# A decoder block over 32 batches: the first LayerNorm's x is loaded already turned, its row statistics go through DRAM to all partitions, GpSimd applies them a batch ahead, and the steps of a batch stand in a new order

## The reference, cut to what matters

```python
# x: (32, 224, 512), ctx: (32, 750, 512); all weights 512 x 512 unless said
def _layernorm(x): return (x - mean(x)) / sqrt(var(x) + 1e-5)       # over the last axis, no weights
def attn(x):                                                        # 16 heads of 32
    q = x @ Wq.T / sqrt(512); k = x @ Wk.T; v = x @ Wv.T
    return concat_heads(softmax(q k^T) v) @ Wff.T + bff
def xattn(ctx, q):  ...  # one head over 750 rows of ctx
def ffn(h):         ...  # routing to 2048 keys, top 8, gathered values, a learned gate
x = x + attn(_layernorm(x))
x = x + xattn(ctx, _layernorm(x))
x = x + ffn(_layernorm(x))
```

## Time and profile before

| what | value |
|---|---|
| median of 3 runs | 2862.47 us (2859.62 to 2865.25) |
| the profiled execution, its time | 2859.07 us |
| the same, from its first to its last instruction (span) | 2857.2 us |
| busy: TensorE, VectorE, ScalarE, GpSimd | 2649.0, 2104.9, 1421.1, 785.7 us |
| mean granted clock of TensorE | 0.973 of full speed |

### The profile page before, as it was taken

The page is one execution under the profiler, slowest core; times in us unless marked ns, Lnnn a source line. Parts: engine busy times, 40 slices in busy tenths (PEclk is TensorE's granted clock), DMA queues, the critical chain, the costliest instruction groups (busy, mean ns, idle before and its releaser), DMA issues.

```text
span 2857.2 us, 53958 instructions
## 1 busy us (share of the span) xinstructions
PE 2649.0 (93%) x18042; PEld 1983.5 (69%) x18042; DVE 2104.9 (74%) x4071; ACT 1421.1 (50%) x4214; POOL 785.7 (27%) x651
## 2 busy tenths in 40 slices
PE   6899999999999999999999999999999999999830
PEld 4667777777777777777777777777777777777610
DVE  4446778878777788877777878777788877777652
ACT  2345554445455444555554445455544455555343
POOL 0001323222223232222323222223232222233245
PEclk9999999999999999999999999999999999999965
DMA  5112323333333332333323333333332333333799
GB/s 167 57 57 76 103 91 118 103 102 105 107 101 100 102 120 86 108 107 109 103 91 116 110 96 104 107 101 104 99 120 89 107 107 110 101 93 108 180 237 181
DMA packets 102683, 313.05 MB, mean 110 GB/s; under 512 B 14577, under 2 KB 15089, under 8 KB 94417
## 3 DMA queue, kind: packets, MB, share of 16 engines
q1 hardware_dynamic: 54002, 180.37, 19.2%
q0 software_dynamic: 48640, 132.16, 17.4%
HBM read 269.35 MB, written 43.12 MB: 109 GB/s over the span
## 4 chain that ended last, share of the span: by engine, by line
PE 90%; issue 2%; DVE 2%; DMA 2%; ACT 1%; POOL 1%; SPq 1%; POOLq 0%; DVEq 0%; ACTq 0%
PE psX L985 45%; PE psA L985 19%; PE psF L985 8%; PE psA L994 8%; PE psA L1072 4%; PE psA L1049 4%; PE psX L994 3%; DMA vg<-in_L_ffn_aux_values,idx 1%; DVE xT_lo L775 1%; PE psF L994 1%; ACT xT_hi L567 1%; POOL out L540 1%; POOL vg L523 0%; SPq L371 0%; ACT paT L550 0%
## 5 line engine op out<-in xcount | busy, mean ns | idle before, releaser
L523 POOL DMA_INDIRECT vg<-in_L_ffn_aux_values,idx x512 | 516.5, 1009 | 1635.1 <-DVE agg L890 830.9
L586 ACT ACTIVATE pa<-psA,nmax 112x224 f32<-112x224 f32 x1024 | 443.6, 449 | 150.3 <-DVE nmax L794 147.6
L890 DVE SCALAR_TENSOR_TENSOR agg<-vg,wt,agg 112x512 f32<-112x512 f32 x420 | 367.5, 875 | 16.2 <-DMA vg<-in_L_ffn_aux_values,idx 2.9
L794 DVE TENSOR_REDUCE nmax<-psA 112x4 f32<-112x896 f32 x256 | 266.7, 1083 | 149.8 <-PE psA L1049 149.8
L985 PE MATMUL psX<-big,gT 128*112 128x375 f32 x1024 | 333.4, 478 | 1.3 <-ACT nx L622 1.0
L985 PE MATMUL psX<-pT,cx 125*128 125x224 f32 x1536 | 307.5, 357 | 0.0
L550 ACT COPY paT<-psA 112x448 f32<-112x448 f32 x512 | 236.5, 544 | 111.1 <-PE psA L994 108.7
L985 PEld LDWEIGHTS psX<-pT,cx 125*128 125x128 f32 x1536 | 285.5, 190 | 7.7 <-issue 0.3
L807 DVE TENSOR_TENSOR pa<-pa,rsum 112x896 f32<-112x896 f32 x256 | 279.5, 1092 | 8.8
L985 PEld LDWEIGHTS psX<-big,gT 128*112 128x112 f32 x1024 | 177.4, 176 | 127.1 <-ACT nx L622 1.2
L985 PE MATMUL psX<-m,xnxT 128*112 128x512 f32 x512 | 235.6, 603 | 0.0
(11 more groups left out here) (195 smaller groups left out, 5301.5 us busy)
## 6 DMA issues: line engine op xcount, KB each, us to landing
big<-in_ctx_t SPq DMA_DIRECT2D x32, 1500.0 KB, 6.7
cx<-in_ctx SPq DMA_DIRECT2D x32, 1500.0 KB
xa<-in_x SPq DMA_DIRECT2D x32, 448.0 KB, 4.7
xr<-in_x SPq DMA_DIRECT2D x32, 448.0 KB, 3.9
out<-x SPq DMA_DIRECT2D x32, 448.0 KB, 3.1
agg_scratch<-agg SPq DMA_DIRECT2D x60, 224.0 KB, 6.4
vg<-in_L_ffn_aux_values,idx POOLq DMA_INDIRECT x512, 3.7
over_weights<-agg_scratch SPq DMA_DIRECT2D x15, 448.0 KB, 13.5
```

The costliest lines, as they stand in the source:

```text
L523: pool.indirect_dma_start(vg[:, c % SLOTS, k, :], None, aux_values, bass.IndirectOffsetOnAxis(ap=idx[:, t, n:n + 1], axis=0))\
L586: last = nc.scalar.activation(pa[:, t, h, :], psA[0:R, h, t * S:(t + 1) * S], ACT.Exp, bias=nmax[:, k % 2, h, t:t + 1], accum_out=rsum[:, ...
L794: nc.vector.tensor_reduce(nmax[:, k % 2, h:h + 2, :], psA[0:R, h:h + 2, 0:T * S].rearrange("p h (t s) -> p h t s", t=T), AX_X, ALU.max, ne ...
L890: last = nc.vector.scalar_tensor_tensor(dst, vg[:, c % SLOTS, k, :], w, dst, ALU.mult, ALU.add)
```

## The change

- x is passed a second time, turned: `in_x_t`, per batch 128 partitions x 896 (four chunks of 224 rows). SyncE loads it into a new buffer `centered`.
- A new stream N works on batch i + 1. ("N", "norm"): VectorE's statistics as before, without the last two operations (centring and scaling 112x512); then two small copies put mean and inverse root into `moments`, which SyncE stores to DRAM. ("N", "spread"): SyncE loads these 448 numbers into all 128 partitions (`spread`). ("N", "center"): GpSimd subtracts the mean and multiplies by the inverse root over 128x896 values, in place, ScalarE writes the high part and VectorE the low part, one operation each.
- TensorE's turn of `xa` is gone, and with it two fills. So that the fills stay a multiple of four, ("A", "value") now has four: each is 12 matmuls with 256 columns instead of 512.
- `ORDER` is new. A list `FIRST` puts ahead of iteration 0: norm and spread of batch 0, the split of Wq, its centring, then the split of Wk and Wv, then the keys. Iteration 30 is unrolled too.

```diff
-    ("A", "norm", 0), ("X", "enter", 0), ("A", "turn", 0), ("G", "sum", 0), ("X", "norm", 0), ("A", "qk", 0),
...
+    ("G", "sum", 0), ("X", "enter", 0), ("X", "norm", 0), ("A", "qk", 0), ("A", "value", 0), ("G", "sum", 1),
...
-FILLS = {("A", "turn"): 2, ("A", "qk"): 1, ("A", "value"): 2, ("A", "score"): HB, ("A", "prob"): 2 * T,
+FILLS = {("A", "qk"): 1, ("A", "value"): 2 * T, ("A", "score"): HB, ("A", "prob"): 2 * T,
...
+FIRST = (("N", "norm", 0), ("N", "spread", 0), ("W", "split", 0), ("N", "center", 0), ("W", "split", 1),
+         ("W", "split", 2), ("W", "keys", 0), ("W", "keys", 1), ("W", "keys", 2), ("W", "keys", 3))
...
+            def store_moments(b, _):
+                sp.wait_ge(moments_ready, b + 1)
+                sp.dma_start(row(moments_dram, b), moments[:, :, :].rearrange("p t k -> p (t k)")).then_inc(moments_stored, 16)
+                if not (isinstance(b, int) and b == B - 1):
+                    sp.dma_start(xa[:, :, :], tiles(row(x, b + 1))).then_inc(x_loaded, 16)
+
+            def spread_moments(b, _):
+                sp.wait_ge(moments_stored, 16 * (b + 1))
+                wait(sp, xt_scaled, b)
+                sp.dma_start(spread[:, :], row(moments_dram, b).rearrange("r k -> (r k)").partition_broadcast(P))\
+                    .then_inc(moments_spread, 16)
...
+            def center(b, _):
+                mean, rstd = (spread[:, :].rearrange("p (r t k) -> p k t r", t=T, k=2)[:, k, :, :].unsqueeze(1)
+                              .to_broadcast([P, C, T, R]) for k in range(2))
+                xt = centered[:, :, :].rearrange("p c (t r) -> p c t r", t=T)
+                pool.wait_ge(xt_loaded, 16 * (b + 1))
+                pool.wait_ge(moments_spread, 16 * (b + 1))
+                nc.gpsimd.tensor_tensor(xt, xt, mean, ALU.subtract).then_inc(mean_taken, 1)
+                pool.wait_ge(mean_taken, b + 1)
+                nc.gpsimd.tensor_tensor(xt, xt, rstd, ALU.mult).then_inc(xt_scaled, 1)
...
-            def a_norm(b, _):
+            def x_moments(b, _):
                 dve.wait_ge(x_loaded, 16 * (b + 1))
-                norm("A", b, xa, xa, xa_normed)
+                statistics("N", b, xa, rstd["N"][:, :])
+                assert count["N"] == N_STEPS
+                wait(dve, moments_stored, 16 * b)
+                nc.vector.tensor_copy(moments[:, :, 0], mv["N"][:, :, 0])
+                nc.vector.tensor_copy(moments[:, :, 1], rstd["N"][:, :]).then_inc(moments_ready, 1)
...
+            def center_lo(b, _):
+                dve.wait_ge(xT_hi, b + 1)
+                lo(xT[1][:, :, :], centered[:, :, :], xT[0][:, :, :]).then_inc(xT_split, 1)
```

More of the change, by code:

```diff
@@ L162, in build @@
         xa = sb("xa", [R, T, D])
+        moments = sb("moments", [R, T, 2])
+        spread = sb("spread", [P, R * T * 2])
+        centered = sb("centered", [P, C, S])
         xT = (sb("xT_hi", [P, C, S], F32R), sb("xT_lo", [P, C, S], F32R))
@@ L243, in build @@
         small_loaded, mask_loaded = sem("small_loaded"), sem("mask_loaded")
-        steps = {s: sem(f"dve_step_{s}") for s in "AXFG"}
+        steps = {s: sem(f"dve_step_{s}") for s in "NAXFG"}
         log_done, lsum_spread, mean_full = sem("log_done"), sem("lsum_spread"), sem("mean_full")
@@ L302, in iteration @@
                         step[s, name](b, arg)
+            for s, name, arg in FIRST:
+                if (s, name) in step:
+                    step[s, name](0, arg)
             for i in range(3):
                 iteration(i)
-            with eng.Fori(3, B - 1) as i:
+            with eng.Fori(3, B - 2) as i:
                 iteration(i)
+            iteration(B - 2)
             iteration(B - 1)
@@ L341, in build, with flat @@
         SMALL, LOOK_UPS = 9, 4
+        def flat(w):
+            return w[:, :, :].rearrange("p c s -> p (c s)")
         def rows_of(w):
@@ L478, in _ @@
                           ("W", "cb"): first_cxT, ("W", "gb"): first_ctx,
-                          ("X", "score"): next_cxT, ("X", "mix"): next_ctx, ("A", "turn"): next_x, ("X", "enter"): next_xr,
+                          ("X", "score"): next_cxT, ("X", "mix"): next_ctx, ("N", "norm"): store_moments,
+                          ("N", "spread"): spread_moments, ("N", "center"): next_xt, ("X", "enter"): next_xr,
                           ("F", "norm"): store_base,
@@ L560, in turn, with center_hi @@
                 return step
-            def turn_hi(b, _):
-                for j in range(2):
-                    job = FILL["A", "turn", 0] + j
-                    wait_full(act, "A", job, b)
-                    nc.scalar.copy(xT[0][:, 2 * j:2 * j + 2, :], chunks("A", job)).then_inc(xT_hi, 1)
+            def center_hi(b, _):
+                act.wait_ge(xt_scaled, b + 1)
+                wait_full(act, "A", max(FILL["A", "value", 0] + 2 * T - 1, FILL["A", "qk", NB - 1]), b - 1)
+                nc.scalar.copy(xT[0][:, :, :], centered[:, :, :]).then_inc(xT_hi, 1)
             def qk(b, k):
@@ L575, in value @@
                 for t in range(T):
-                    j = FILL["A", "value", 0] + t
-                    copy_out("A", j, b, va[:, t, :, :], bank("A", j)[0:R, :].rearrange("p (h d) -> p h d", h=H))
+                    for half in range(2):
+                        j = FILL["A", "value", 0] + 2 * t + half
+                        copy_out("A", j, b, va[:, t, half * H // 2:(half + 1) * H // 2, :],
+                                 bank("A", j)[0:R, 0:D // 2].rearrange("p (h d) -> p h d", d=DH))
             def exp_scores(b, k):
@@ L775, in lo @@
                 return nc.vector.tensor_tensor(dst, src, hi.bitcast(F32), ALU.subtract)
-            def turn_lo(b, _):
-                for j in range(2):
-                    job = FILL["A", "turn", 0] + j
-                    dve.wait_ge(xT_hi, 2 * b + j + 1)
-                    part = slice(2 * j, 2 * j + 2)
-                    lo(xT[1][:, part, :], bank("A", job)[:, 0:2 * S].rearrange("p (c s) -> p c s", c=2), xT[0][:, part, :])\
-                        .then_inc(drained["A"][job % banks["A"]], 1)
+            def center_lo(b, _):
+                dve.wait_ge(xT_hi, b + 1)
+                lo(xT[1][:, :, :], centered[:, :, :], xT[0][:, :, :]).then_inc(xT_split, 1)
             def qk(b, k):
@@ L798, in share @@
             def share(b, k):
+                if k == 0:
+                    count["A"] = 0
                 for t in range(T):
@@ L1022, in qk @@
                         pe.wait_ge(split, 2 * C)
-                    wait_drained(pe, "A", FILL["A", "turn", 0] + 1, b)
+                    pe.wait_ge(xT_split, b + 1)
                 j = FILL["A", "qk", k]
@@ L1033, in value @@
                     pe.wait_ge(split, 3 * C)
-                wait_drained(pe, "A", FILL["A", "turn", 0] + 1, b)
+                pe.wait_ge(xT_split, b + 1)
                 for t in range(T):
-                    j = FILL["A", "value", 0] + t
-                    wait_free(pe, "A", j, b)
-                    filled("A", j, product3(bank("A", j)[0:R, :], [(both(xT, ALL, c, slice(t * R, (t + 1) * R)),
-                                                                    both(wvT, ALL, c, ALL)) for c in range(C)]))
+                    for half in range(2):
+                        j, cols = FILL["A", "value", 0] + 2 * t + half, slice(half * D // 2, (half + 1) * D // 2)
+                        wait_free(pe, "A", j, b)
+                        filled("A", j, product3(bank("A", j)[0:R, 0:D // 2],
+                                                [(both(xT, ALL, c, slice(t * R, (t + 1) * R)), both(wvT, ALL, c, cols))
+                                                 for c in range(C)]))
             def scores(b, k):
```

101 lines of the change are left out of this document (57 added, 44 removed), and 24 rows, old and new, of tables (ORDER, SETUP).

## The result

The changed kernel takes 3018.23 us (median of 4 runs, 3009.34 to 3028.47), the kernel before 2862.95: 1.0544 times the time, 95% interval 1.0501 to 1.0588. Forecast were 2888, in a range of 2812 to 2914. The sign was right, the size was not: +155 us where +29 stood.

The account below looks back on a forecast made before the run. TensorE, 93% busy, was taken to bound the kernel, with one repeating wait, for `xT_lo`. Iterations 3 to 30 gave +25.2 us, three others -5.1, the beginning +9.1: +29 on 2859.1 makes 2888 us, range 2812 to 2914.

Parts of the forecast that it names:

- The turn and value: TensorE per iteration: the turn's wait and transposes go, -2.41 us; `value` with 48 smaller matmuls costs +0.41 us.
- the straight line: `value`: interpolated between measured matmuls, 256 columns take 0.125 us each, so 48 take 5.99 us instead of 5.58.
- my lower bound: `value`: added cost of 0 if matmuls with half the columns cost half the time.
- The hold by `bias_x`: GpSimd's addition holds VectorE's statistics, ending 2.4 us late; TensorE waits 2.6 us per iteration at ("A", "prob", 1) and ("X", "prob", 0).
- The step from a wide operation and a tiny one: VectorE: two forms seen held beside GpSimd's addition, so the statistics' 112x2 operations with two SBUF inputs are held too.
- The centring: GpSimd, 4.2 us from some 57 us into the iteration; just misses `share` 2 at 60 us, so no cost.
- TensorE's slack there: At `share` 2: TensorE has about 2 us to spare if VectorE is held.
- The rival with this mechanism: Centring also meets `share` 2, holding VectorE up to another 2.1 us per iteration: 2947 us, chance 0.07.
- The clock: TensorE's granted clock: the forecast had no term for it, 0 us.
- The new order: Other new places in the loop: at most 0.1 us at ("A", "prob", 0) and 0.2 at ("A", "prob", 3), +0.3 per iteration.
- The beginning: Before the loop: ("A", "qk", 0) starts at 40.5 us, 14.2 later; +9.1 us net (from 0 to +16).
- the first rival: VectorE is not held beside `bias_x`, the wait is 0.2 us: -38 us, 2821 us, chance 0.31.

Follow-up runs that it names:

- The best version: Changed kernel with addition and centring later, a shorter beginning with `spread` at once, and the old order from `value` 0 to F's `turn`: 2822.99 us.
- the two edits: Changed kernel with `bias_x` started later (2954.63 us), or the centring held until the last `share` is done (2956.47 us); both together 2855.76 us.
- The last experiment: Version with both pieces later and a shorter beginning (2842.25 us), with the steps from `value` 0 to F's `turn` in their old order: 2822.99 us.
- the version with both pieces later: Changed kernel with `bias_x` beside the maxima of the fourth scores and the centring beside F top 0: 2855.76 us.

## Why the prediction was right or wrong

**The turn and value: right.** The wait and the transposes disappeared as counted (-2.40 us), and `value` cost 0.13 us where I had 0.41. I took the straight line between 224 and 512 columns; my lower bound was nearer. The best version's iteration, 1.69 us under before, is what remains of this gain.

**The hold by `bias_x`: right in mechanism, place and size.** Forecast were 2.6 us per iteration at ("A", "prob", 1) and ("X", "prob", 0) for `qk_lo` and `nx`; it was 1.20 + 1.13. Moving the addition gave 63 us. The step from a wide operation and a tiny one with a pointer scalar to tiny ones with two inputs from SBUF held for three further forms: 112x2 in the statistics (2.92 us), 112x2 in `xrec` (0.86 for 0.14), and the share multiplication. So far the rule of the Trainium skill (SBUF — State Buffer, "Who interferes with whom") agrees, that a VectorE instruction with two SBUF inputs contends with a GpSimd instruction that reads SBUF.

**The centring: this is the largest step that failed.** The prediction says: "The centring, 2 x 2.39 x 896 / 1024 = 4.2 us on GpSimd, starts behind the last gathers, some 57 us into the iteration by my count", "`share` 2 begins 60 us in. I take it that they just miss each other." These numbers contradict the conclusion: 57 + 4.2 is 61.2, past 60. Then three terms went the wrong way. The centring starts 59.4 us in (1398.48 against ("X", "enter") at 1339.1; `share` 2 begins at 1399.93, 60.8 us in), since `spread` lands 8.5 us after its issue, behind the next `xa` and the 1.5 MB of turned ctx. Its operations take 2.54 us alone, not 2.1: fewer elements than the addition, but more time. And I had put TensorE's slack there at about 2 us; of 2.5 us of hold, 1.9 reached it. The rival with this mechanism named 2947 us and got 0.07; by my own two numbers it should have had the larger part.

**The clock: missing.** No term of the sum had it. The kernel before shows 1.00 in its loop with a wait of 1.43 us per iteration, and I took that as given. With four waits in an iteration it falls in 19 of 25 iterations and costs 1.4 us per iteration on average, 40 us in all. This is the larger part of why the two edits, 63 and 62 us apart, gave 162 together.

**The new order: partly.** "No wait beyond 0.1 us" at ("A", "prob", 0) was wrong: prob fills the bank whose low part VectorE has just been given to read, 0.65 us, and the transposes of all four prob steps went slower by 0.83 us together. In the loop that is 1.48 us where I had 0.3, and 0.1 more in `value`. That the bank of the low part makes the transposes slower, and not only wait, is argued and not shown. The last experiment returned 0.87 of it by the order alone.

**The beginning: right at its first point, 41.4 for 40.5,** and too small after it (+13 us at iteration 3, where the forecast's terms make about +6).

**The sum.** Per iteration I missed 1.9 (centring), 1.4 (clock) and 1.3 (order), 4.6 us, and gained 0.5 on `value` and the hold. By the iterations as measured, those from 3 to 30 took 110 us more than forecast (+135 for +25), the beginning 7 to 8 and the end 4: together the 121 us by which the profiled execution (3009.3 us) passed the forecast.

The centring is the largest single term, but it is not enough. With it out of the way and the forecast's own hold left, the kernel takes 2956 us, 68 above the forecast and still outside its range: the clock and the order, put at 0 and 0.3, would have failed it alone.

Two slips of the working changed nothing. The terms named for the beginning (32, 4.2, 1.0, 1.0 and 2.5) make 40.7 and not 40.5. And the forecast's own range, 2868 to 2912, follows from the bounds of `value` and of the beginning, not of the hold: with nothing held the sum is the first rival's 2821.

## What to carry to other kernels

Work that is moved to GpSimd has a second price, paid by VectorE: list what VectorE does in the whole stretch from its earliest to its latest start, and give the piece a place where VectorE works from PSUM (in the version with both pieces later, two row maxima from 921.84 took 2.09 us together beside the addition of 921.90 to 924.25, as long as without it) or has slack. When two pieces of a count are said to miss each other, write both ends down and compare them; if they lie within a microsecond or two, the case where they meet is the likely one. And if a change adds waits, count TensorE's clock as a term: in a version with two defects mending either alone can look like less than half of what mending both is worth.

## What the runs showed of the hardware that I had not expected

- The held operation can be the one that seems to start first: L778 is shown from 1470.81, the addition from 1471.33, and still L778 ends with the addition. The Trainium skill (SBUF — State Buffer, "Who interferes with whom") says that the one that issues first gets the shared ports for the whole instruction; by these starts the trace does not agree. It is so in all 28 iterations, by 0.5 us. The gather that GpSimd shows until 1471.31 is not what holds L778: with the addition moved away, no such operation took over 0.23 us beside the same gathers. A start in the profile may not be the moment that counts, which no run here can tell.
- GpSimd's centring, 128x896 with an operand that is read with a stride and repeated, takes 2.54 us; its addition over 112x1024 takes 2.37. The time does not follow the number of elements per partition alone.
- The hold goes both ways: beside the share multiplication GpSimd's second operation takes 3.28 us instead of 2.52.
- The moments' store landed 1.4 us after its issue in the loop; the spread of the same 1.8 KB to 128 partitions (224 KB written) took 3.1 us at best, 5.3 behind 0.45 MB and 8.5 behind 1.5 MB more.
